# A two-layer graph network: residual tiles, a dense table and the first graph's entry dealt anew

## The reference

```
h = relu(layernorm(x))
x = x + attention(h, adj)          # 16 heads of 32, mask adj == 0 -> -inf, softmax, then @ Wo + bo
h = relu(layernorm(x))
q, k, o = h @ wq, h @ wk, h @ weight
alpha = relu(q @ k.T) * (adj != 0)  # 256 x 256
x = x + softmax(alpha, axis=1) @ o
```

## Time and profile before

| | us |
|---|---|
| three runs, median (lowest, highest) | 1922.4 (1921.23, 1922.53) |
| profiled execution, its own time | 1918.12 |
| its span, first to last instruction | 1916.3 |
| mean granted clock of TensorE | 0.99 |
| busy: PE, DVE, ACT, POOL | 1779.5, 1620.9, 1087.8, 452.0 |

### The profile page before, as it was taken

How to read it: one execution, slowest core, us unless ns; L and a number is a source line. 1 busy time by engine, 2 the same in 40 slices (tenths; PEclk the granted TensorE clock), 3 DMA queues, 4 the chain that set the end, 5 groups by cost and what they waited for, 6 DMA issues and landing times.

```text
span 1916.3 us, 53466 instructions
## 1 busy us (share of the span) xinstructions
PE 1779.5 (93%) x16817; PEld 1404.2 (73%) x16817; DVE 1620.9 (85%) x4904; ACT 1087.8 (57%) x2381; POOL 452.0 (24%) x1190
## 2 busy tenths in 40 slices
PE   3789999999999999999999999999999999999986
PEld 2557777777777777777777777777777777777763
DVE  5688888988888898888888888888888888888884
ACT  2356555656565555656566565656565656656551
POOL 1022221222122222222122222212221222222111
PEclk9899999999999999999999999999999999999998
DMA  3412122222222222222222221222222222222121
GB/s 109 139 53 77 50 84 81 81 70 78 74 58 80 84 69 78 79 59 74 79 86 67 79 79 51 82 82 71 79 79 68 65 78 85 68 79 79 44 58 39
DMA packets 195401, 142.48 MB, mean 74 GB/s; under 512 B 36000, under 2 KB 167072, under 8 KB 195360
## 3 DMA queue, kind: packets, MB, share of 16 engines
q1 hardware_dynamic: 178224, 108.93, 19.9%
q10 hardware_dynamic: 17136, 33.03, 5.5%
HBM read 57.94 MB, written 16.78 MB: 39 GB/s over the span
## 4 chain that ended last, share of the span: by engine, by line
PE 50%; DVE 28%; issue 8%; DMA 6%; ACT 5%; SPq 1%; ACTq 1%; DVEq 1%; POOL 0%; POOLq 0%
PE ring L360 34%; PE turned L425 6%; DVE probs L792 6%; DMA out_dram<-x 5%; ACT probs L588 3%; PE score L410 3%; DVE probs_t_lo L800 3%; DVE x L930 2%; DVE val L891 2%; PE ring L478 2%; PE pv L443 2%; DVE work L859 2%; DVE o_sum L813 2%; DVE xa L859 2%; DVE e_lo L951 1%
## 5 line engine op out<-in xcount | busy, mean ns | idle before, releaser
L598 ACT ACTIVATE probs_t_hi<-turned 128x512 f16<-128x512 f32 x512 | 304.7, 595 | 371.5 <-PE turned L425 336.9
L588 ACT ACTIVATE probs<-probs,least 128x256 f32<-128x256 f32 x1024 | 461.3, 503 | 10.8 <-DVE least L792 10.8
L792 DVE CUSTOM_DVE_ANT_0 probs<-score,far,undo_score 128x256 f32<-128x256 f32 x1024 | 450.5, 478 | 9.6 <-DVE far L978 9.6
L1081 POOL TENSOR_TENSOR heads_out<-o_sum,o_rcp 128x64 f32<-128x64 f32 x512 | 144.6, 303 | 1150.3 <-DVE o_sum L813 1141.1
L800 DVE TENSOR_TENSOR probs_t_lo<-turned,probs_t_hi 128x512 f16<-128x512 f32 x512 | 350.3, 684 | 50.8 <-ACT probs_t_hi L598 47.3
L425 PE MATMUL turned<-ident,probs 128*128 128x128 f32 x2048 | 311.6, 275 | 42.7 <-ACT probs L588 42.7
L425 PEld LDWEIGHTS turned<-ident,probs 128*128 128x128 f32 x2048 | 244.6, 142 | 89.1 <-ACT probs L588 53.3
L410 PE MATMUL score<-stack 128*128 128x256 f16 x1024 | 197.1, 274 | 16.4 <-DMA stack<-stage 16.4
L443 PE MATMUL pv<-val,probs_t_hi 128*128 128x65 f16 x2048 | 184.7, 191 | 4.6 <-DVE o_sum L813 2.7
L445 PE MATMUL pv<-val,probs_t_lo 128*128 128x33 f16 x2048 | 178.2, 179 | 0.0
L443 PEld LDWEIGHTS pv<-val,probs_t_hi 128*128 128x128 f16 x2048 | 157.8, 97 | 11.7 <-DVE probs_t_lo L800 5.6
(11 more groups left out here) (160 smaller groups left out, 4307.8 us busy)
## 6 DMA issues: line engine op xcount, KB each, us to landing
stack<-stage SPq DMA_DIRECT2D x2048, 32.0 KB, 1.9
x<-x_dram ACTq DMA_DIRECT2D x32, 512.0 KB, 4.4
out_dram<-x SPq DMA_DIRECT2D x32, 512.0 KB, 2.9
xa<-x_dram ACTq DMA_DIRECT2D x31, 512.0 KB, 3.7
adj_in<-adj_dram SPq DMA_DIRECT2D x32, 256.0 KB, 2.9
adjt_in<-adj_t_dram SPq DMA_DIRECT2D x32, 256.0 KB, 3.0
wq_raw<-wq_dram SPq DMA_DIRECT2D x2, 512.0 KB, 6.2
wk_raw<-wk_dram SPq DMA_DIRECT2D x2, 512.0 KB, 7.9
```

The lines of the kernel that those rows point to most:

```text
L588: last = nc.scalar.activation(probs[:, u % 2, q, :], probs[:, u % 2, q, :], ACT.Exp, bias=least[:, u % 2, q:q + 1], scale=-1.0)
L598: nc.scalar.activation(pH[:, u % 2, :, :], turned[u % 2][:].rearrange("p (k n) -> p k n", k=QT), ACT.Copy).then_inc(hi["p"], 1)
L792: last = nc.vector.tensor_tensor_reduce(out=probs[:, u % 2, q, :], in0=score[u % 2][:, q * NODES:(q + 1) * NODES], in1=far[:, q, :], scale ...
L1081: last = nc.gpsimd.tensor_tensor(dst, o_sum[:, pair % 2, q:q + 3:2, :], o_rcp[:, pair % 2, q:q + 3:2].unsqueeze(2).broadcast_to([P, 2, HEAD]),
```

## The change

- **Residual tiles.** `av0` and `av1` are taken out by ACT (scaled, into a new buffer `xo`), and POOL adds x1 (`residual`, step 15). x is loaded into a new buffer `xin` in step 4 of the graph's own body; POOL's bias addition reads `xin` and writes `x1`. The store reads `xo` and is issued in the next body behind the stacks of heads 4 to 7.
- **Second softmax.** `e_lo` leaves DVE: POOL multiplies (two of 128x256) and subtracts (one of 128x512) in step 13.
- **First layer norm.** Its statistics move to steps 9 and 10, the reciprocal deviation on POOL to step 10, with a 16th step (minus_mean), and the normalising to POOL, step 13; `far_next` moves to step 11.
- **Dense table.** `v1` is halved over steps 5 and 6, `h2` stands in step 6, `g0` ahead of `h1` in step 7, `g1` in 8, `hw0` in 11, `qk1` whole in 13, `av0` and `av1` in 14, `v0` whole in 15. On DVE `sum_parts` of the last pair goes ahead of `turned_low(0)`.
- **Entry.** The first scale is found after the first transposes, weights are split in body -1, wv's scale is found after `qk0`, body -1's scores stand after its dense tiles; the late weights are issued in two parts, behind the stacks of heads 4 to 7 and of heads 8 to 11 of graph 0; the last weights are split three a step from step 14.

```diff
-NSTEPS = (3 + 4 * NEWTON_ROUNDS, 2 + 3 * NEWTON_ROUNDS)
+NSTEPS = (4 + 4 * NEWTON_ROUNDS, 2 + 3 * NEWTON_ROUNDS)
...
     ["qk3"],
-    ["v1", "h2_0", "h2_1"],
-    ["h1_0", "h1_1", "g0"],
+    ["v1a"],
+    ["h2_0", "h2_1", "v1b"],
+    ["g0", "h1_0", "h1_1"],
     ["g1"],
-    ["hw0"],
     ["qk0"],
     ["al"],
-    ["v0a"],
+    ["hw0"],
     ["hw1"],
-    ["v0b", "av0"],
-    ["av1", "qk1a"],
-    ["ot0", "qk1b"],
+    ["qk1"],
+    ["av0", "av1"],
+    ["ot0", "v0"],
 ]
...
-STATS1, VAR1, NORM1 = (7, 9), 9, 12
+STATS1, VAR1, NORM1 = (9, 10), 10, 13
...
-X1_STEP, KEEP_STEP, FAR_STEP = 1, 3, 10
+X1_STEP, XIN_STEP, KEEP_STEP, FAR_STEP = 1, 4, 3, 11
+FINAL = (15, 15)
...
+LATE = {1: ("wk1_t", "wq1_t"), 2: ("wo", "w1")}
...
-                   "av0": (final, 2, 0), "av1": (final, 2, 1),
+                   "av0": (weighed, 2, 0), "av1": (weighed, 2, 1),
...
                 if cur:
                     stack_heads(1, t)
+                    if not prev:
+                        load_late(1)
+                if prev and started(p - 1):
+                    store(p - 1)
+                if cur:
                     stack_heads(2, t)
+                    if not prev:
+                        load_late(2)
                     stack_heads(3, t)
...
-                if prev:
-                    sp.wait_ge(final, count(p, 2, 1))
-                    sp.dma_start(out_v[p, :, :, :], x1[:]).then_inc(stored, 16)
+
+            def store(b):
+                sp.wait_ge(final, count(b, 2, 1))
+                sp.dma_start(out_v[b, :, :, :], xo[:]).then_inc(stored, 16)
...
+                elif name.startswith("av"):
+                    act.wait_ge(mm["av"], count(b, 2, k))
+                    if k == 0 and started(b - 1):
+                        act.wait_ge(stored, count(b - 1, 16, 15))
+                    nc.scalar.activation(xo[:, k, :], src[:], ACT.Copy, scale=undo_final[:, 0:1]
+                                         ).then_inc(weighed, 1)
...
-                if prev:
-                    if started(p - 1):
-                        act.wait_ge(stored, count(p - 1, 16, 15))
-                    act.dma_start(x1[:], x_v[p, :, :, :]).then_inc(x1_in, 16)
                 for s in range(HEADS):
+                    if cur and s == XIN_STEP:
+                        if prev:
+                            act.wait_ge(x1_ok, count(p, 1, 0))
+                        act.dma_start(xin[:], x_v[t, :, :, :]).then_inc(x1_in, 16)
...
-                if s == AL_STEP + 3:
-                    dve.wait_ge(hi["e"], count(b, 1, 0))
-                    for m in range(QT):
-                        last = nc.vector.scalar_tensor_tensor(
-                            out=eL[:, m, :], in0=work[:, 1, m * NODES:(m + 1) * NODES],
-                            scalar=l1_rcp[:, m:m + 1], in1=eH[:, m, :],
-                            op0=ALU.mult, op1=ALU.subtract)
-                    last.then_inc(lo["e"], 1)
...
+                step(nc.gpsimd.tensor_scalar(minus_mean[:], meanvar[0][:, :, 0], -1.0, None,
+                                             ALU.mult))
...
+            def first_normalise(b):
+                pool.wait_ge(nstep[0], count(b, NSTEPS[0], NSTEPS[0] - 1))
+                settle(pool, pool_settled)
+                for q in range(QT):
+                    nc.gpsimd.tensor_scalar(xa[:, q, :], xa[:, q, :], minus_mean[:, q:q + 1],
+                                            rstd[0][:, q:q + 1], ALU.add, ALU.mult
+                                            ).then_inc(normed[0], 1)
+
+            def second_softmax(b):
+                pool.wait_ge(hi["e"], count(b, 1, 0))
+                settle(pool, pool_settled)
+                for m in range(QT):
+                    part = work[:, 1, m * NODES:(m + 1) * NODES]
+                    last = nc.gpsimd.tensor_scalar(part, part, l1_rcp[:, m:m + 1], None, ALU.mult)
+                last.then_inc(e_ok, 1)
+                pool.wait_ge(e_ok, count(b, 1, 0))
+                settle(pool, pool_settled)
+                nc.gpsimd.tensor_tensor(eL[:].rearrange("p m n -> p (m n)"), work[:, 1, :],
+                                        eH[:].rearrange("p m n -> p (m n)"), ALU.subtract
+                                        ).then_inc(lo["e"], 1)
+
+            def residual(k, b):
+                pool.wait_ge(weighed, count(b, 2, k))
+                nc.gpsimd.tensor_tensor(xo[:, k, :], xo[:, k, :], x1[:, k, :], ALU.add
+                                        ).then_inc(final, 1)
...
+                    if s == AL_STEP + 3 and prev:
+                        second_softmax(p)
+                    if s == NORM1 and later:
+                        first_normalise(n + 1)
+                    for k in range(QT):
+                        if s == FINAL[k] and prev:
+                            residual(k, p)
...
                     if s == X1_STEP and prev:
+                        if started(p - 1):
+                            pool.wait_ge(final, count(p - 1, 2, 1))
                         pool.wait_ge(x1_in, count(p, 16, 15))
                         for q in range(QT):
-                            last = nc.gpsimd.tensor_tensor(x1[:, q, :], x1[:, q, :], out_bias[:],
+                            last = nc.gpsimd.tensor_tensor(x1[:, q, :], xin[:, q, :], out_bias[:],
                                                            ALU.add)
...
-                    if s == FAR_STEP and nxt:
+                    if s == (FAR_STEP if cur else 0) and nxt:
```

More of the change, by code:

```diff
@@ L164, in two_layers @@
         x1 = sb("x1", [P, QT, DIM], f32)
+        xo = sb("xo", [P, QT, DIM], f32)
+        xin = sb("xin", [P, QT, DIM], f32)
         adj_in = sb("adj_in", [P, QT, NODES], i32)
@@ L199, in two_layers @@
         rstd = [sb(f"rstd{n}", [P, QT], f32) for n in (1, 2)]
+        minus_mean = sb("minus_mean", [P, QT], f32)
         newton = [sb(f"newton{n}", [P, 3, QT], f32) for n in (1, 2)]
@@ L309, in _, with load_late @@
                     load_raw(sp, name, half)
+            def load_late(g):
+                for name in LATE[g]:
+                    for half in range(2):
+                        load_raw(sp, name, half)
             def stack_heads(g, b):
@@ L338, in body @@
                     stack_heads(0, n)
-                if nxt and not cur:
-                    for name in LOADS[EARLY // 2:]:
-                        for half in range(2):
-                            load_raw(sp, name, half)
-                if prev:
-                    sp.wait_ge(final, count(p, 2, 1))
-                    sp.dma_start(out_v[p, :, :, :], x1[:]).then_inc(stored, 16)
+            def store(b):
+                sp.wait_ge(final, count(b, 2, 1))
+                sp.dma_start(out_v[b, :, :, :], xo[:]).then_inc(stored, 16)
             sweep(sp, body)
+            store(BATCH - 1)
             sp.wait_ge(stored, 16 * BATCH)
@@ L566, in body @@
                     if nxt and not cur and s == step_of("h1_1"):
+                        find_scale(0, 2, pv)
+                    if nxt and not cur and s == step_of("qk0"):
                         find_scale(1, 1, pv)
+                    if nxt and not cur and s + AHEAD >= HEADS:
+                        scores(s + AHEAD - HEADS, t + 1)
             for name in ORDER:
                 assert len({bank_before(name, t) for t in range(2, BATCH - 2)}) == 1
-            find_scale(0, 2, pv)
             sweep(pe, body)
@@ L578, in split_high @@
                 nc.scalar.activation(high, src, ACT.Copy, scale=by).then_inc(w_high, 1)
-            act.wait_ge(scaled, 1)
-            for c in range(FIRST):
-                split_high(c)
             def exponentials(u, b):
@@ L697, in body @@
                     if nxt and not cur and s == step_of("h1_1"):
+                        act.wait_ge(scaled, 1)
+                        for c in range(FIRST):
+                            split_high(c)
+                    if nxt and not cur and s == step_of("qk0"):
                         act.wait_ge(scaled, 2)
@@ L984, in body @@
                         first_stats(STATS1.index(s), n + 1)
-                    if s == NORM1 and cur and later:
-                        normalise(0, xa, xa, n + 1)
                     for name in DENSE[s]:
@@ L992, in body @@
                     if nxt and not cur and s == step_of("h1_1"):
+                        for c in range(FIRST):
+                            split_low(c)
+                    if nxt and not cur and s == step_of("qk0"):
                         for half in range(2):
@@ L1002, in body @@
                     if cur and not prev and s >= LAST_SCALE_STEP:
-                        at = EARLY + 2 * (s - LAST_SCALE_STEP)
-                        for c in range(at, at + 2):
+                        at = EARLY + 3 * (s - LAST_SCALE_STEP)
+                        for c in range(at, at + 3):
                             split_low(c)
-                if later and not cur:
-                    normalise(0, xa, xa, n + 1)
             for q in range(QT):
```

(3 more changed lines are left out.)

36 lines of the change are left out of this document (16 added, 20 removed).

## The result

The changed kernel takes 2036.1 us (four runs, 2035.15 to 2036.85), the kernel before 1922.5 (four runs, 1921.23 to 1923.33): ratio 1.059, 95% interval 1.057 to 1.061. The forecast was 2022, in a range of 1958 to 2088, slower with 0.90. The profiled execution took 2035.93, its span is 2034.1, and its mean granted clock 0.971 in place of 0.99.

What follows compares the result with a forecast made beforehand. TensorE, busy 93% of the span, was taken as the bound. Terms of +3.7 us per graph over 29 graphs (+108), with -8 at entry and exit, took 1918.1 to 2018; 4.3 for the median gave 2022, range 1958 to 2088.

Steps and rivals of the forecast that it cites:

- step 0, wait of ACT gone, 0.1 back: Head of the loop: ACT no longer waits for the stored output; 1.38 us per graph won, 0.1 kept for ACT's next work.
- step 1: `ot1` waited for POOL's last heads, held late by the same store and x1 wait; 0.28 us per graph won.
- steps 5 to 7, the table: The dealt tiles leave PE waiting for DVE: 3.0 us of waits where before had 1.2, +1.8 per graph.
- `av0` waits for `e_lo`: POOL's queue from step 10 finishes the second softmax late, so PE waits 2.7 us per graph (2.2 to 3.4).
- the clock: PE gaps bring a fall of the granted clock in 7 of 10 graphs; +1.05 us per graph (0 to 2).
- Less on VectorE: DVE loses six instructions a graph, none behind step 4 where it is short; PE moves by nothing.
- the same waits and a clock that holds: Rival: the loop's waits come as forecast without clock falls; +69, 1991 us, chance 0.25.
- Entry: Up to step 2 of graph 1: stack wait goes, DVE then waits for wo; -7 us (0 to -12).
- Exit: DVE's x1 wait goes, 1.8 on the path; last residual through ACT and POOL +1.3; softmax evens out; -1 us.
- both waits absent: Rival: neither the `av0` wait nor those of steps 4 to 7 appear; 1862 us, chance 0.03.
- late at `av0` and with steps 5 to 7 as before: Rival: POOL late but steps 4 to 7 not, DVE reaching head 5 sooner; 1970 us, chance 0.10.
- with the wait at `av0` taken away by moving `e_lo`: Matched to the rival that POOL is in time and `av0` doesn't wait; 1914 us, chance 0.05.

Runs made afterwards that it cites:

- e5_xin: The kernel before with only x loaded into its own buffer in step 4 and GpSimd waiting for the store: 1894.2 us, ratio 0.9864.
- e9_xin_sum: e5_xin with VectorE's sum of the last two heads put ahead of turned_low of head 0: 1888.8 us, ratio 0.9824 to the kernel before.
- e2_elo_dve: The changed kernel with e_lo back on VectorE as one fused instruction a tile: 1916.4 us, ratio 0.9971 to the kernel before.
- e3_table: The changed kernel with v1 whole and both h2 in step 5, both h1 in step 6, g0 alone in step 7: 1968.4 us.
- e11_two_ops: The changed kernel with GpSimd's softmax multiplication given a second operation, plus 0.0, same values: 1986.0 us, ratio 1.0344 to the kernel before.
- e1_far9: The changed kernel with far_next in step 9 in place of step 11: 1936.7 us.
- e4_fill: The changed kernel with 22 purposeless matmuls of 256 columns ahead of av0's wait for e_lo: 2005.9 us.
- e7_top9: e6_mend with VectorE's maxima of wo and w1 four steps later in the first graph: 1860.7 us, ratio 0.9694 to the kernel before.
- e8_mend_dve: The changed kernel with steps 5 to 7 as in e3_table, e_lo on VectorE, wo and w1 maxima four steps later: 1857.7 us, ratio 0.9675 to before.
- e6_mend: The changed kernel with e3_table's table, first statistics in steps 7 and 9, reciprocal deviation in 9, far_next in 8: 1868.9 us, ratio 0.9735 to before.
- e10_order: e8_mend_dve with hw0 in step 9, al in step 10 and qk0 in step 11: 1858.6 us, ratio 0.9674 to the kernel before.

## Why the prediction was right

Step by step, in us per graph, forecast and measured:

| step of the prediction | forecast | measured |
|---|---|---|
| step 0, wait of ACT gone, 0.1 back | -1.28 | -1.40 |
| step 1 | -0.28 | -0.21 |
| step 13, `av0` no more there | -0.27 | -0.28 |
| steps 5 to 7, the table | +1.8 | +1.75 |
| `av0` waits for `e_lo` | +2.7 | +2.95 |
| the clock | +1.05 | +1.16 |
| sum | +3.7 | +3.97 (the periods: +3.94) |

**The x1 part** gave its gain. The 0.1 kept for ACT's v pass and exponentials was not needed: step 0 is 2.19 against 2.18 of work. The reason given for step 1 was wrong, and that its size was right is luck: the heads weren't late for the x1 wait but for VectorE's order (e5_xin, e9_xin_sum), which the prediction passed over. In e9_xin_sum, without the new place of `qk1`, 0.34 of the gain turned up again as a wait for stacks.

**Less on VectorE** is worth nothing, as argued: 84 us off it gave nothing, and e2_elo_dve put `e_lo` back on it at no loss.

**The table.** With 0.87 for turn, scores and weigh, 0.44 for an h1 or h2 tile and 1.31 for half a product, steps 5 to 7 hold 2.18, 3.06 and 4.38 of work and took 12.61: 2.99 is lost, against the 3.0 forecast. The timeline shows 0.68, 0.79 and 0.93 of it as gaps, at the three places named. e3_table took 1.45 of it back.

**GpSimd's chain.** Its start was foreseen at T10 + 5.0 and its second softmax at T10 + 14.6; with T10 at 342.47 they came at 5.0 and 14.5. The chain up to there was made of durations from rows, and it held. Inside the softmax the multiplication took 0.92 where 0.72 was taken (bounds 0.45 and 1.08) and the subtraction 1.15 where 1.27 was, +0.27 in all, about the 0.25 by which the wait is longer than forecast. So two errors partly cancel here. The prediction took the row of far_next for the same operation; it is the same kind of instruction, but with two operations, from int32 (L1162: a comparison and a multiplication). Its 1.08 lay nearer to the 0.92 than the 0.72 did, but e11_two_ops shows that this was no reason: the form with one operation is slow, and with two on float32 the multiplication takes 0.48, near the lower bound of 0.45. The range of the prediction held, its choice within the range had no ground in either row. That `av0` waited for this, and for nothing else, is shown by e1_far9 and e2_elo_dve.

**The clock** fell in 21 of 29 graphs (forecast 7 in 10) and cost 1.16 a graph. e4_fill shows it as a cost of its own, which stands on the gap: 30 us. The rival with the same waits and a clock that holds is thus the time of e4_fill, 2005.9, 15 above the 1991 that was worked out for it: 5 of these lie between entry and exit, 12.6 at entry and exit together, and 3.4 go off because the forecast set the median 4.3 above the profiled execution, where e4_fill has 0.9.

**Entry:** -7 forecast (0 to -12), -1.4 measured to step 2 of graph 1. The wait for wo was foreseen at the right place (VectorE reaches it at 64 and gets it at 71.5, forecast 61 and 72), and e7_top9 shows its price, 8 us. The gap at weigh of head 6 was 4.66, shorter than the 9 forecast. What comes behind it was taken too hopefully: among others the first merge, of 8 matmuls, took 5.41 at a mean granted clock of 0.68, where before it took 3.60 at 1.00. Those single terms weren't tried.

**Exit:** -1 forecast, +5.6 measured, the term that was wrong. Read from one tile of PE to the next, beside the kernel before: `g0` starts 1.6 earlier (the x1 wait, forecast 1.8); it takes 1.3 longer, at the lower clock; PE waits 1.4 in front of `g1`; from `g1` to `av0` it is 1.5 more, nearly all of it GpSimd's softmax; and from `av0` to the end 2.9 more, of which the residual over two engines is 1.3, as forecast (e8_mend_dve, whose clock stays up through `av0`, has 1.3 more there than before), and the rest the clock. So the waits of the dealt order, the softmax and the clock were put at nothing. "The softmax evens out" was no calculation: from the end of `e_hi` to that of `e_lo` GpSimd takes 3.4, VectorE 2.0, though `hw1`'s low half stands ahead of it. By the prediction's own durations GpSimd takes 2.9, so 0.9 of the 1.4 could have been had. Only the difference of the engines at the `av0` wait is clean (3.74 against 2.36). Whole exits aren't: e2_elo_dve has `e_lo` on VectorE and still takes 50.6, since its clock fell once more, during wo's tiles, for 1.4.

**The whole.** The forecast was 14 too low: 6 in the loop, 12 at entry and exit, less 4, since the changed kernel's median lies 0.2 and not 4.3 above its profiled execution. The upper end of the range was added up wrongly: 6 a graph and -1 at the exit give 2095, not 2090. Nothing hangs on it.

**The other rivals.** They are no mere figures. e6_mend is "both waits absent", with the changed kernel's parts on the same engines: 1868.9 beside the 1862 worked out for that case. e3_table, late at `av0` and with steps 5 to 7 as before, is at 1968.4 beside 1970, and e2_elo_dve, with the wait at `av0` taken away by moving `e_lo`, at 1916.4 beside 1914.

## What to carry to other kernels

Where an instruction goes to an engine that is idle for three quarters of the span, lay out that engine's own queue up to it and count every instruction ahead, with its start: here one conversion of 2.14 us in the wrong step cost 99 us. What is freed on an engine that ends no wait is worth nothing, however many microseconds it is. And when a bound kernel loses little waits in several places, undo them one at a time before the change is thrown away: the same parts, with three tiles and a few step numbers set otherwise (e6_mend, e7_top9), are 3% faster than the kernel before.

## What the runs showed of the hardware

**On GpSimd the form of an instruction can count more than its size.** One operation on 128x256 took 922 ns, the same with a second operation 480 (the changed kernel and e11_two_ops differ in nothing else), and two operations on 128x512 763 to 813. The type counts as well: `far_next`, two operations on 128x256 from int32, took 1071 to 1083 ns in every kernel but e10_order (1182). The Trainium skill (GPSIMD Engine Reference, section 3.1) gives about 1.8 cycles an element at best, 768 ns for 512. The float32 rows with two operations agree for 512 and are a quarter above the rule for 256 (384 ns, an estimate from that page); the row with one operation is over twice it.

**A copy on VectorE waited for GpSimd.** The same copy, in the changed kernel, where it starts at 359.27 beside `e_lo`, and in e1_far9, where it starts at 348.75 and `e_lo` has ended at 347.36 (groups by form, mean ns behind the comma):

```profile
L989 DVE COPY far<-far_next 128x512 bf16<-128x512 bf16 x32 | 30.0, 938 | 0.0
```

```profile
L989 DVE COPY far<-far_next 128x512 bf16<-128x512 bf16 x32 | 9.1, 286 | 0.0
```

In the graph above it ends at 360.27, 0.15 behind GpSimd's `e_lo`. The Trainium skill (SBUF — State Buffer, "Who interferes with whom") says that a VectorE instruction in a mode with two ports and one of GpSimd exclude each other for the whole instruction; the trace agrees for `e_lo`, which began first, but doesn't show that nothing at all overlaps: the copy ends 0.15 behind it and takes 0.28 alone. And in e11_two_ops the copy takes 0.28 though GpSimd's normalising of `xa` is recorded as begun 0.03 ahead of it; there it is GpSimd that is slower, 0.87 in place of the 0.76 of e1_far9. No step of PE grew for the copy: steps 13 and 15 are as long as in e1_far9.

**With smaller gaps ahead of a large one the clock fell more often.** The gap of 2.8 was followed by a fall of the clock in 21 of 29 graphs with three gaps of 0.7 to 0.9 ahead of it, and in 8 of 29 with smaller ones (e3_table). One of 1.9 with the three ahead of it was followed by a fall in 6 of 29 (e11_two_ops), one of 0.54 in none (e1_far9). A fall cost 1.7: in the loop of the changed kernel the period is 60.9 with one and 59.2 without. Where it fell, this stretch behind `av0` of one graph shows it (columns as in the earlier trace rows):

```profile
301.00:306.50 5.50, 5.50 (x39) 3.95 (x38) 1.66 (x6) 3.14 (x6) 2.80 (x4) 0.72 0.19 49
```
